# A graph-attention layer on one Trainium2 core: weighted sums from three bf16 parts of scaled rows, and h spread by one fp32 product a tile

## What is computed

```python
h = x @ Watt.T + Watt_b
e = leaky_relu(sum(h[dst] * tanh(h[src] + edge_attr), -1) / 8)     # one score an edge
p = exp(e - segment_max(e, dst)[dst])
h_neigh = segment_sum(x[src] * p / (segment_sum(p, dst)[dst] + 1e-9), dst)
out = leaky_relu((x + h_neigh) @ W1.T + b1 + (x * h_neigh) @ W2.T + b2)
y = layernorm(x + out)
```

## Time and profile before

| | |
|---|---|
| median of 3 runs | 3102.68 us (3100.49 to 3104.06) |
| the profiled execution | 3100.4 us |
| its span | 3098.6 us |
| mean granted TensorE clock | 0.536 of full speed |
| gathers in the main part | 1631, 945 ns each |

### The profile page before, as it was taken

The page is one execution under the profiler, slowest core; times in us unless marked ns, Lnnn a source line. Parts: engine busy times, 40 slices in busy tenths (PEclk is TensorE's granted clock), DMA queues, the critical chain, the costliest instruction groups (busy, mean ns, idle before and its releaser), DMA issues.

```text
span 3098.6 us, 45175 instructions
## 1 busy us (share of the span) xinstructions
PE 1502.2 (48%) x11423; PEld 1295.1 (42%) x11423; DVE 1290.4 (42%) x7378; ACT 1364.1 (44%) x3900; POOL 1570.8 (51%) x1670
## 2 busy tenths in 40 slices
PE   4255444454444444544445444445444445444456
PEld 4244443444433444433444444444443344444345
DVE  2343444444444444434444444444434444344445
ACT  2244444444444444444444444444444444444446
POOL 4454455555555555455554555555555555555551
PEclk7555555555555555555555555555555555555555
DMA  4112222222222222222222222222222222222221
GB/s 169 51 52 59 58 59 56 60 59 60 58 59 61 55 59 59 58 59 61 55 59 58 59 58 61 55 59 59 59 58 61 61 54 59 59 58 61 61 60 30
DMA packets 169471, 187.26 MB, mean 60 GB/s; under 512 B 126146, under 2 KB 126358, under 8 KB 169315
## 3 DMA queue, kind: packets, MB, share of 16 engines
q0 software_dynamic: 53152, 107.98, 13.9%
q1 hardware_dynamic: 114897, 76.96, 9.0%
q10 hardware_dynamic: 1266, 0.93, 0.1%
HBM read 175.64 MB, written 10.07 MB: 60 GB/s over the span
## 4 chain that ended last, share of the span: by engine, by line
issue 50%; PE 47%; another core or an unknown queue 1%; DVE 1%; ACT 0%; DVEq 0%; POOL 0%; POOLq 0%
PE ps_acc L991 21%; PE ps_hd L945 13%; PE ps_hot L930 6%; PE ps_acc L1007 2%; PE ps_row L957 2%; PE ps_misc L972 1%; PE ps_acc L990 1%; PE ps_spare L998 1%; PE ps_misc L1002 1%; DVE hx L1151 0%; PE ps_row L898 0%; PE ps_row L894 0%; ACT hotT L730 0%; ACT weight L777 0%
## 5 line engine op out<-in xcount | busy, mean ns | idle before, releaser
L632 POOL DMA_INDIRECT got<-table,src_i x1631 | 1541.3, 945 | 1461.6 <-PE ps_acc L991 964.1
L945 PE MATMUL ps_hd<-h,hotT 128*128 128x64 bf16 x4983 | 410.3, 238 | 1371.6 <-issue 1370.5
L945 PEld LDWEIGHTS ps_hd<-h,hotT 128*128 128x128 bf16 x4983 | 328.7, 130 | 1457.4 <-issue 1456.1
L730 ACT ACTIVATE hotT<-ps_hot 128x1024 bf16<-128x1024 bf16 x222 | 211.9, 955 | 1387.5 <-PE ps_hot L930 1387.5
L991 PE MATMUL ps_acc<-got,weight 128*128 128x65 f32 x3322 | 706.8, 380 | 1.6 <-ACT weight L777 1.6
L991 PEld LDWEIGHTS ps_acc<-got,weight 128*128 128x128 f32 x3322 | 663.4, 294 | 54.0 <-issue 38.6
L777 ACT ACTIVATE weight<-hot,arg 128x128 f32<-128x128 bf16 x1661 | 507.3, 386 | 102.6 <-issue 64.3
L1244 DVE CUSTOM_DVE_ANT_0 edge<-edge,ps_hd 128x64 f32<-128x64 f32 x1661 | 265.0, 217 | 687.1 <-issue 430.1
L1233 DVE TENSOR_TENSOR edge<-edge,got 128x256 f32<-128x256 f32 (+1 forms) x444 | 179.4, 404 | 407.6 <-remote 278.6
L747 ACT ACTIVATE edge<-edge 128x256 f32<-128x256 f32 (+1 forms) x444 | 166.6, 394 | 133.3 <-issue 85.4
L930 PE MATMUL ps_hot<-ident,hot 128*128 128x128 bf16 x1661 | 198.0, 312 | 2.9 <-DVE hot L1222 2.9
(11 more groups left out here) (134 smaller groups left out, 1375.9 us busy)
## 6 DMA issues: line engine op xcount, KB each, us to landing
edge<-in_edge_attr SPq DMA_DIRECT2D x110, 480.0 KB
got<-table,src_i POOLq DMA_INDIRECT x1631
table<-hx SPq DMA_DIRECT2D x12, 512.0 KB
hw<-table SPq DMA_DIRECT2D x111, 32.0 KB
xw<-in_x SPq DMA_DIRECT2D x111, 32.0 KB, 1.9
out<-y_out SPq DMA_DIRECT2D x111, 32.0 KB
x_piece<-in_x SPq DMA_DIRECT2D x3, 768.0 KB, 4.3
row_i<-in_dst SPq DMA_DIRECT2D x110, 1.0 KB
```

Of the source, the lines that this page charges most:

```text
L632: pool.indirect_dma_start(got[b.four][:, g, 0:2 * D], None, table, bass.IndirectOffsetOnAxis(ap=src_i[b.four][:, g:g + 1], axis=0))\
L730: act.activation(hotT[b.two][:, a:z, :], ps, ACT.Copy, bias=1.0, scale=-1.0).then_inc(hot_sb[p], 1)
L945: last = pe.matmul(expanded(g), hotT[b.two][:, g, :], h3[b.two][:, part, :], start=(part == 0), stop=(part == 2))
```

## The change

Two things change.

**Spreading h.** `expand` multiplies h itself (`hw`, fp32) with a one-hot in fp32 (`hotT` now has fp32 buffers): one product a tile instead of three. `split_h` goes away on ACT (two instructions a window) and on DVE (two). The scale 1/8 moves into `dot`. The one-hot is built as one where edge and node meet, and `copy_hot` copies without scale and bias.

**Weighted sums.** ACT takes one Exp over `arg` (128x15) instead of 15 over 128x128. DVE multiplies the gathered [x, 1] rows of a piece with it (`scale_rows`), and the result is split into three bf16 parts: ACT copies it to bf16 (`high_part`), DVE subtracts (`left_part`), ACT copies the rest to bf16 (`mid_part`), DVE subtracts again (`low_part`). Each function runs twice a window, once for each piece. PE then multiplies the bf16 one-hot with the three parts side by side: one bf16 product of 195 columns a tile. DVE adds the three parts with a reduce from PSUM in place of the copy L1302.

With that, waits and orders move. The gathers wait for `scale_rows` of window n-4 and no longer for PE's sum; `load_h` waits for the second `hd_ready`; `build_hot` waits for the sum and not for the last weights. PE's sum is done in two pieces, ahead of `lay_rows`, and behind the carry. The core of the diff:

```diff
-                    for part in range(3):
-                        last = pe.matmul(expanded(g), hotT[b.two][:, g, :], h3[b.two][:, part, :],
-                                         start=(part == 0), stop=(part == 2))
+                    last = pe.matmul(expanded(g), hotT[b.two][:, g, :], hw[b.two][:, :], start=True, stop=True)
...
-                for g in range(*cols(b, c)):
-                    last = act.activation(weight[:, g, :], hot[b.four][:, g, :], ACT.Exp,
-                                          bias=arg[:, g:g + 1], scale=-MASKED)
-                last.then_inc(weights_done[c], 1)
+            def probabilities(b):
+
+                act.wait_ge(arg_done, b.n + 1)
+                act.activation(prob[:, 0:tiles(b)], arg[:, 0:tiles(b)], ACT.Exp).then_inc(prob_set, 1)
+
+            def high_part(b, p):
+                a, z = piece(b, p)
+                act.wait_ge(scaled[p], b.n + 1)
+                if follows(b, 1):
+
+                    act.wait_ge(summed[p], b.n)
+                if p == NP - 1 and carried(b):
+
+                    act.activation(carry_weight[:, :], carry_arg[:, :], ACT.Exp)
+                act.activation(parts[:, a:z, 0, :], rest[:, a:z, :], ACT.Copy).then_inc(rest_high[p], 1)
+
+            def mid_part(b, p):
+                a, z = piece(b, p)
+                act.wait_ge(rest_left[p], b.n + 1)
+                act.activation(parts[:, a:z, 1, :], rest[:, a:z, :], ACT.Copy).then_inc(rest_mid[p], 1)
...
-                    last = pe.matmul(a_sum, weight[:, g, :], got[b.four][:, g, D:2 * D + 1],
+                    last = pe.matmul(a_parts, hot[b.four][:, g, :], parts[:, g, :, :].rearrange("p a d -> p (a d)"),
                                      start=(g == 0), stop=(g == tiles(b) - 1))
-                if c % 2 == 1:
-                    last.then_inc(summed[c // 2], 1)
+                last.then_inc(summed[p], 1)
...
+            def scale_rows(b, p):
+                a, z = piece(b, p)
+                dve.wait_ge(prob_set, b.n + 1)
+                dve.tensor_tensor(rest[:, a:z, :], got[b.four][:, a:z, D:2 * D + 1],
+                                  prob[:, a:z].rearrange("p (g d) -> p g d", d=1).to_broadcast([P, z - a, D + 1]),
+                                  ALU.mult).then_inc(scaled[p], 1)
+
+            def left_part(b, p):
+                a, z = piece(b, p)
+                dve.wait_ge(rest_high[p], b.n + 1)
+                dve.tensor_tensor(rest[:, a:z, :], rest[:, a:z, :], parts[:, a:z, 0, :], ALU.subtract)\
+                    .then_inc(rest_left[p], 1)
+
+            def low_part(b, p):
+                a, z = piece(b, p)
+                dve.wait_ge(rest_mid[p], b.n + 1)
+                dve.tensor_tensor(parts[:, a:z, 2, :], rest[:, a:z, :], parts[:, a:z, 1, :], ALU.subtract)\
+                    .then_inc(rest_low[p], 1)
```

More of the change, by code:

```diff
@@ L162, in gnn_layer @@
         hw = [sb(f"hw{k}", [P, D]) for k in range(2)]
-        h_left = sb("h_left", [P, D])
-        h3 = [sb(f"h3_{k}", [P, 3, D], BF16) for k in range(2)]
         xw = [sb(f"xw{k}", [P, D]) for k in range(BUFS)]
@@ L167, in gnn_layer @@
         hot = [sb(f"hot{k}", [P, TILES, P], BF16) for k in range(BUFS)]
-        hotT = [sb(f"hotT{k}", [P, TILES, P], BF16) for k in range(2)]
+        hotT = [sb(f"hotT{k}", [P, TILES, P]) for k in range(2)]
         raw = [sb(f"raw{k}", [P, TILES]) for k in range(2)]
@@ L190, in gnn_layer @@
         arg = sb("arg", [P, TILES])
-        weight = sb("weight", [P, TILES, P])
+        prob = sb("prob", [P, TILES])
+        spare = sb("spare", [P, TILES * P])
+        parts = sb("parts", [P, TILES, 3, D + 1], BF16)
         sums = sb("sums", [P, D + 1])
@@ L207, in gnn_layer @@
         y_old = sb("y_old", [P, D])
-        spare = weight[:, :, :].rearrange("p g n -> p (g n)")
+        rest = spare[:, 0:TILES * (D + 1)].rearrange("p (g d) -> p g d", d=D + 1)
         rows_i = spare[:, 0:SEARCH_ROW].bitcast(I32)
@@ L728, in copy_hot @@
                         act.wait_ge(carry_ps, b.n - (BUFS - 1))
-                    act.activation(sel[b.four][:, :], ps[:, z - a - 1, P - 1:P], ACT.Copy, bias=1.0, scale=-1.0)
-                act.activation(hotT[b.two][:, a:z, :], ps, ACT.Copy, bias=1.0, scale=-1.0).then_inc(hot_sb[p], 1)
-            def split_h(b, part):
-                if part == 0:
-                    act.wait_ge(h_in[b.two], (b.twos + 1) * 16)
-                    if follows(b, 2):
-                        act.wait_ge(hd_ready[NP - 1], b.n - 1)
-                    act.activation(h3[b.two][:, 0, :], hw[b.two][:, :], ACT.Copy, scale=SCALE).then_inc(h_high, 1)
-                else:
-                    act.wait_ge(h_left_set, b.n + 1)
-                    act.activation(h3[b.two][:, 1, :], h_left[:, :], ACT.Copy).then_inc(h_mid, 1)
+                    act.activation(sel[b.four][:, :], ps[:, z - a - 1, P - 1:P], ACT.Copy)
+                act.activation(hotT[b.two][:, a:z, :], ps, ACT.Copy).then_inc(hot_sb[p], 1)
             def tanh(b, c):
@@ L822, in step @@
                     copy_carry(before)
+                if exists(b):
+                    tanh(b, 2)
+                    tanh(b, 3)
                 if exists(third):
@@ L983, in sum_edges @@
                         pe.wait_ge(own["z1"], b.n - 1)
-                pe.wait_ge(weights_done[c], b.n + 1)
-                for g in range(*cols(b, c)):
+                pe.wait_ge(rest_low[p], b.n + 1)
+                for g in range(*piece(b, p)):
                     if g == tiles(b) - 1 and carried(b):
@@ L1378, in step @@
                     finish_nodes(third)
-                if exists(nxt):
-                    split_h(nxt, 0)
                 if exists(b):
@@ L1384, in step @@
                     dot(b, 0)
+                if exists(prev):
+                    left_part(prev, 0)
+                    left_part(prev, 1)
+                if exists(b):
                     add(b, 2)
                     dot(b, 1)
-                if exists(nxt):
-                    split_h(nxt, 1)
+                if exists(prev):
+                    low_part(prev, 0)
+                if exists(prev):
+                    low_part(prev, 1)
                 if exists(b):
```

106 lines of the change are left out of this document (46 added, 60 removed).

## The result

The changed kernel takes 2953.45 us (2950.71 to 2964.11, 4 runs) against 3102.29 (3100.49 to 3104.06): the ratio is 0.9527, 95% interval 0.9502 to 0.9551. It is faster by 149 us, where 3217 us and a loss had been forecast. The profiled execution has a span of 2950.0 us.

What follows compares the result with a forecast made beforehand. Bound: a cycle of waits between gather bursts, no engine full. A window: 21.4 + 1.8 + 2.7 + 1.7 + 0.8 = 28.4 us against 27.33; 1.07 x 107 = 114 us on 3102.7 gives 3217 us, range 3000 to 3450.

Steps and rivals of the forecast that it cites:

- slow stretch: While POOL gathers, other engines crawl from about 5 us after the first gather; ends 21.4 us after it, bound to gathers.
- The Trainium skill's rule of the prediction: PE: fast weight load needs 128 weights not in fp32, so the new spreading pays the fp32 price, 6.8 us a window.
- The gate: What a window's gathers wait for: `src_i` instead of PE's sum, since the scaling of window n-4 is long past.
- R: The moment all engines are at full speed again, 21.4 us after a window's first gather.
- The choice between the two cases: SP's 12 instructions done at R, 26.7 us a window, or all behind R, 28.4 us; the upper was chosen.
- SP's 12 instructions: Small SP instructions between store and next load L483: 15.87 us in the slow stretch, 1.78 us without gathers.
- DVE's 7 further instructions: DVE instructions newly falling into the slow stretch and so behind R, some 0.2 us each, pushing `y_out` by 1.5 us.
- the case that I chose: All 12 SP instructions behind R: 28.4 us a window, 3217 us; forecast range 3120 to 3300, chance 0.42.
- the push: Late DVE instructions delay `y_out` by 1.5 us, more then fall behind R the next time, so the delay feeds itself.
- rival A: Faster: SP's instructions and DVE's step fit into the slow stretch, 26.7 or 26.2 us a window, 3035 to 2980; chance 0.30.
- rival B: Much slower: `y_out` itself falls behind R, 29.2 to 32 us a window, 3300 to 3600 us; chance 0.19.
- Rival D: DVE's new fp32 operations hold POOL's gathers, lengthening the slow stretch by 1.3 us, 139 us more: 3356 us; chance 0.04.

Runs made afterwards that it cites:

- narrow: Changed kernel with gathers of half the bytes (x alone, zeros for h of the sources): 2913.82 us in one execution.
- pad kernels: Changed kernel plus a memset nobody reads behind each gather: 128 columns 2869.6 us, 192 columns 2809.66, 256 columns 2612.57, 384 columns 2764.07.
- sums_only: Changed kernel with the spreading of h turned back to three bf16 products a tile; new sums and gate stay: 2943.87 us, ratio 0.9495.
- expand_only: Kernel before with only the spreading of h changed (one fp32 product a tile, no split); old sums, weights and gate: 2995.5 us, ratio 0.9662.
- gate_sums: Changed kernel with gathers waiting again for PE's sums of window n-4 instead of DVE's scaling: 3232.32 us, ratio 1.0419.
- idx_mid: Changed kernel with SP's src_i and dst_i loads moved behind the edge load, ahead of the row's and x's: 2972.34 us, ratio 0.9599.
- idx_early: Changed kernel with SP's src_i and dst_i loads moved ahead of the edge, row and x loads: 2981.83 us, ratio 0.9598.
- before_pad2: Kernel before with a memset of 256 columns behind each gather, one each 1.44 us: 2981.96 us, ratio 0.9606.

## Why the prediction was wrong

**What bounds the kernel: right.** A cycle of waits from one burst of gathers to the next, with PE's sum as its last step, and a slow stretch from which all engines come out together. Its length of 21.4 us in one window is 21.3 in the mean before and 21.4 after, though PE issued 60 instructions a window less: at this spacing it is not set by the others' instruction count. That it is bound to the gathers I had taken for likely; narrow and the pad kernels show that it hangs on how closely they are issued.

**Sizes: right.** A bf16 product of 195 columns 0.175 us (0.18 forecast); the fp32 spreading 6.61 us a window (6.8); DVE's new operations 660 ns in the mean (660 and 600); ACT's copies 602 and 617 (520 to 600, a little low). The Trainium skill's rule of the prediction, TensorE: Matmul & The Clock Gate, weight-path perf modes, was borne out with the fp32 price of 0.44 us a tile (6.61 / 15). Where it lay, in the slow stretch, it cost next to nothing: 30 records ran on without a stall, and the kernel is some 10 us slower than sums_only, which spreads h the old way.

**The gate: right in kind, mis-sized.** `src_i` did take PE's place. I put the gathers at R + 5.3 if SP is ready at R. It was R + 4.4 in the mean (25.69 - 21.3). The term at fault is SP's way from R to the `src_i` load: 2.85 us by the one window I had read, and 2.0 in the mean after, because the edge load came 19.9 us after the first gather in the mean, 1.4 before R. It had been 2.3 before already (23.6 - 21.3): the window that I read, 27.96 us long, is the longest of 91 (26.7 to 28.0).

**The choice between the two cases: wrong, and it decided the sign.** I argued that SP's 12 instructions just filled the slow stretch, so that a later store would push them behind R, by up to 1.8 us, and that DVE's 7 further instructions would drag it along. The store did come later, 6.8 us after the first gather against 5.5, less than the 7.5 forecast. `y_out`, put at R + 12, came at R + 10.3 in the mean (25.7 - 21.3 + 5.9), nearly where it had been (10.6): PE had begun its transposes in the slow stretch, so ACT's first copy of `hotT` ended at R + 1.6 (1536.24 against 1534.64) and not at R + 2.6, and the three parts followed it sooner. The argument also doesn't close: the 7.5 us are counted with gathers at R + 5.3, but in the case that I chose they start at R + 7.0, and the store, at R + 12.8, would be 5.8 us behind them, where the 12 instructions had just fitted. And last, SP took 13.1 us to the edge load and not 15.6. I had treated 1.3 us an instruction as a fixed pace. It isn't: from store to edge load SP took 15.6 us before, 14.9 in expand_only, 12.3 in sums_only, 13.1 after and 9.8 in gate_sums. The kernels with four copies on ACT in place of 15 Exps are the quick ones, so ACT's fewer instructions may give SP its turns; no run separates that, and why SP was quicker stays open. With this pace there was no delay to feed the push, and the gain of the gate (rival A, priced at 3035, down to 2980) came through, and more.

**The push itself (rival B): real, but further off.** It decides when the `src_i` load is moved up by 1.7 us or more (idx_mid, idx_early), and it shows as single windows of 39 us among short ones and not as a steady 29 to 32.

**Rival D, DVE holds the gathers: real and small.** Gathers are 31 ns longer in the mean (976 against 945), 0.5 us a window: a wide operation holds at most the one gather that starts while it runs. At 1.25 us of spacing the last gather starts 0.5 us later and R moves by 0.1; at 1.55, where POOL bounds, it is 58 us. I gave it a chance of 0.04 as a loss of 139.

The range reached down to 3000 us since I took 26.2 us a window for the best that the gate could give; it was 25.7.

## What to carry to other kernels

When a wait is moved off an engine, read the next one in line and its slack from many windows, not from one: here it had 1.3 us in the mean (3.7 - 2.4), and that was most of the 1.6 gained a window. A stretch in which every engine waits for "issue" is a resource of its own: find what it hangs on (here the spacing of the gathers) before counting instructions or microseconds on any engine. And when an engine that only issues DMAs outruns the rest, try slowing it down.

## What the runs showed of the hardware

- Indirect gathers of 128 rows issued every 1.25 us slow the instruction streams of PE, DVE and SP to one instruction in 0.7 to 1.4 us, from some 5 us after the first gather until 2.5 (after) to 2.9 us (before) behind the end of the last. Halving the bytes changed the time by 1.3%. At 1.34 and 1.39 us the changed kernel was faster (2870, 2810 us), at 1.44 PE took a pair each 0.74 us and not each 2.8 (before_pad2), and at 1.55 the slowing was gone. What it is that gathers and instruction streams share, no run shows. It isn't tied to the packets that the profile marks as instruction loads: 23 of 91 windows before hold none of the large ones (8 KB), and PE's last stall ends 21.2 to 21.6 us after the first gather in all 91.
- With the changed kernel, a memset of 0.33 us behind each of 1631 gathers, 537 us of added POOL work, made the kernel 341 us faster (2953 to 2613).
- A gather that starts while a DVE operation over 520 or 455 elements runs, with both inputs in SBUF (0.69 and 0.63 us), takes up to 1.46 us and not 0.94: it is held until near that operation's end. One that starts before the operation isn't held.
